# At most three gathers of result rows in flight at the end of a cross-attention and mixture-of-experts kernel

## The reference

```
x = x + xattn(layernorm(x), ctx)            # 32 heads of 16, rms-normalised q and k
xt = layernorm(x)                           # 2048 tokens x 512
gate = xt @ Wr + br;  ids = top_k(gate + gate_bias, 2);  probs = softmax(gate at ids)
u  = xt @ Wup[e] + bup[e]                   # for each of 7 experts, 512 x 512
g  = silu(u @ Wgate[e] + bgate[e]) * u
eo = g @ Wdown[e] + bdown[e]
out = sum over the token's two experts of probs * eo  +  the same three layers with Wsu, Wsg, Wsd
x  = x + out
```

## Time and profile before

| what | value |
| --- | --- |
| median of 3 runs | 1083.45 us (1082.43 to 1084.23) |
| span of the profiled execution, first to last instruction | 1096.4 us |
| PE busy | 1011.1 us, 92% of the span |
| DVE busy | 726.6 us, 66% |
| ACT busy | 475.6 us, 43% |
| POOL busy | 287.0 us, 26% |
| mean granted PE clock | 0.974 |

### The profile page before, as it was taken

The page is one execution under the profiler, slowest core; times in us unless marked ns, Lnnn a source line. Parts: engine busy times, 40 slices in busy tenths (PEclk is TensorE's granted clock), DMA queues, the critical chain, the costliest instruction groups (busy, mean ns, idle before and its releaser), DMA issues.

```text
span 1096.4 us, 20598 instructions
## 1 busy us (share of the span) xinstructions
PE 1011.1 (92%) x7368; PEld 791.9 (72%) x7369; DVE 726.6 (66%) x1686; ACT 475.6 (43%) x670; POOL 287.0 (26%) x194
## 2 busy tenths in 40 slices
PE   3699999998999989999699999999999999999776
PEld 3555556565555665555299899999999899999666
DVE  6677876756676675765456887547474774765378
ACT  2256556545666446656723324233333342432111
POOL 3434444432343433432100010110101010101552
PEclk9899999999999999999879999999999999999889
DMA  9430000010000100000131015424242433332564
GB/s 321 159 116 2 1 1 2 20 59 3 1 1 30 49 3 1 21 20 1 49 136 67 20 32 187 158 69 171 70 174 75 179 120 121 139 90 77 163 193 144
DMA packets 32636, 88.90 MB, mean 81 GB/s; under 512 B 5040, under 2 KB 6576, under 8 KB 29104
## 3 DMA queue, kind: packets, MB, share of 16 engines
q1 hardware_dynamic: 25680, 65.34, 16.3%
q0 software_dynamic: 6880, 22.55, 6.9%
HBM read 65.33 MB, written 22.54 MB: 80 GB/s over the span
## 4 chain that ended last, share of the span: by engine, by line
PE 44%; DVE 4%; another core or an unknown queue 2%; issue 1%; ACT 1%; DVEq 0%; ACTq 0%
PE u_ps L958 14%; PE y_ps L958 13%; PE z_ps L958 13%; PE xt_ps L971 2%; DVE x_sb L1391 1%; PE z_ps L952 1%; DVE g_sb L1332 0%; PE xt_ps L984 0%; DVE u_lo L1320 0%; DVE stats L1174 0%; DVE x_sb L1351 0%; DVE g_hi L1335 0%; ACT u_hi L1093 0%; DVE hot_row L1285 0%
## 5 line engine op out<-in xcount | busy, mean ns | idle before, releaser
L454 ACT ACTIVATE probs<-scores 128x1024 f32<-128x1024 f32 x256 | 247.8, 1030 | 164.7 <-PE scores L332 164.7
L204 POOL TENSOR_TENSOR rsqrt<-mean_sq,power 128x16 f32<-128x16 f32 (+1 forms) x69 | 193.0, 2798 | 312.2 <-DVE mean_sq L556 277.3
L958 PE MATMUL z_ps<-u_hi,w_sb 128*128 128x256 f32 x896 | 167.9, 285 | 2.0 <-DVE u_lo L1320 1.6
L958 PE MATMUL u_ps<-x_hi,w_sb 128*128 128x256 f32 x896 | 165.1, 282 | 4.4 <-issue 2.3
L958 PE MATMUL y_ps<-w_sb,g_hi 128*128 128x512 f32 x448 | 143.9, 402 | 12.6 <-DVE g_lo L1337 8.4
L1093 ACT ACTIVATE u_hi<-u_ps,b_ug 128x256 fp32r<-128x256 f32 x112 | 47.1, 472 | 237.0 <-PE u_ps L958 233.0
L958 PEld LDWEIGHTS u_ps<-x_hi,w_sb 128*128 128x128 f32 x896 | 140.4, 190 | 7.2 <-issue 3.8
L958 PEld LDWEIGHTS z_ps<-u_hi,w_sb 128*128 128x128 f32 x896 | 141.0, 190 | 2.9 <-DVE u_lo L1320 2.0
L344 PE MATMUL o_ps<-probs,v_sb 128*32 128x512 f32 x1024 | 136.4, 604 | 0.5 <-ACT probs L454 0.3
L958 PE MATMUL z_ps<-u_lo,w_sb 128*128 128x256 f32 x448 | 126.3, 282 | 0.1
L958 PE MATMUL u_ps<-x_lo,w_sb 128*128 128x256 f32 x448 | 125.9, 281 | 0.0
(11 more groups left out here) (149 smaller groups left out, 1774.4 us busy)
## 6 DMA issues: line engine op xcount, KB each, us to landing
w_raw<-w_all SPq DMA_DIRECT2D x27, 1024.0 KB, 6.9
y_dram<-y_sb SPq DMA_DIRECT2D x40, 256.0 KB, 2.1
ctx_sb<-ctx_t SPq DMA_DIRECT2D x4, 1024.0 KB, 7.3
out<-x_sb SPq DMA_DIRECT2D x16, 256.0 KB
y_dram<-zeros SPq DMA_DIRECT2D x1, 3584.0 KB, 23.6
x_sb<-x SPq DMA_DIRECT2D x1, 3072.0 KB, 20.1
xn_dram<-xn SPq DMA_DIRECT2D x12, 256.0 KB, 2.1
bd<-b_down SPq DMA_DIRECT2D x9, 256.0 KB, 3.4
```

The costliest lines, as they stand in the source:

```text
L204: nc.gpsimd.tensor_tensor(rsqrt[:, half, 0:width], mean_sq[:, half, 0:width], power[:, 0:width], ALU.pow).then_inc(rsqrt_ready, 1)
L454: nc.scalar.activation(probs[:, s % 2, 2 * a:2 * a + 2, :], scores[:, a], ACT.Exp, scale=float(HD) ** 0.5).then_inc(p_ready, 1)
L958: ins = nc.tensor.matmul(out_ps, stat[a], mov[b], start=(first and a + b == 0), stop=(last and a == 1), skip_group_check=True)
```

## The change

A constant FLYING = 3 is added. In `result(m)`, a gather with m of 3 or more first waits on POOL until gather m - 3 has landed, by that gather's own semaphore. The two `xg` gathers between m = 9 and m = 10 have no such wait. Nothing else is changed.

```diff
@@ -776,6 +776,7 @@
         index = sb("index", [P, 2], INT32)
         yg = w_raw[:].rearrange("p m c n -> p (m c) n")
         RING = 3 * DC
+        FLYING = 3
 
         def two_banks(name):
             return ctx.enter_context(nc.psum_tensor(name, [P, 2, 2, TS], FP32))
@@ -914,6 +915,9 @@
 
                 if m >= RING:
                     pool.wait_ge(added, m - RING + 1)
+                if m >= FLYING:
+                    before = m - FLYING
+                    pool.wait_ge(yg_loaded[before % RING], 16 * (before // RING + 1))
                 nc.gpsimd.indirect_dma_start(
                     out=yg[:, m % RING, :], out_offset=None, in_=y_dram,
                     in_offset=bass.IndirectOffsetOnAxis(
```

## The result

The changed kernel took 1090.65 us as a median of 20 runs (1088.83 to 1096.52), against 1084.16 us for the kernel before (20 runs, 1080.34 to 1090.80). The ratio is 1.0057, interval 1.0044 to 1.0071: slower by 0.6%, or 6.5 us. The forecast was no change, 1083.5 us within 1080.6 to 1086.8, and it was missed.

The account below looks back on a forecast made before the run. The prediction saw a late PE signal to ACT in the closing tiles, taken as hardly present in timed runs. Waits at 0, slip within slack and no stall removed summed to 0 us: 1083.5 us, range 1080.6 to 1086.8.

Parts of the forecast that it names:

- 29 waits at 0, a slip of 0 to 1 us behind 1.6 us of slack: Last stage: POOL's added waits cost nothing and later gathers slip less than their consumers' slack; 0 us in sum.
- L: Time from a gather's start on POOL to its landing; 3.7 to 4.2 us at first, 4.6 to 6 beside stores.
- the first burst: Result gathers m = 0 to 9 in the first closing tile; ten started, 1.7 outstanding, the limit just met.
- rival 2: At m = 3 to 9 and the `xg` pair, the limit paces gathers too slowly; 1085.3 to 1088.3 us, chance 0.20.
- the slip of m = 9: Delay of gather m = 9 under the limit, 3L - 11.6: nothing at 3.7, 1.0 us at 4.2, 3.4 at 5.
- slack of 2.0 us: First closing tile: m = 9 lands at 1036.2, its add starts at 1038.2 in an undisturbed run.
- From m = 14 ... POOL then runs ahead of DVE and the slack grows from tile to tile: Later gathers: the ring's wait on `added` lets POOL go on at once, since adds come 14 us earlier.
- The stall: Closing tiles: PE's `z_ready` reaches ACT 6 and 14 us late while gathers move; 14.4 to 16.7 us of the span.
- It comes with the recording: Claim that profiling causes the late signal, so timed runs hardly have it and nothing is there to be won.
- the subtraction: Profiled span 1096.4 us less timed median 1083.45: at least 12.95 us not in timed runs, at most 3.75 us of stall left.
- undisturbed span: Span of the kernel before without the late signal, put at 1079.7 to 1082.0 us.
- Rival 1: Closing tiles: timed runs have the late signal too and fewer gathers remove it; all gives 1079.7 us, chance 0.18.

Follow-up runs that it names:

- before_quiet: The kernel before, unedited, profiled in a later measurement; 1083.67 us, ratio 1.0010, span 1080.9 us.
- fly3_first: Kernel before plus the limit of three for m = 3 to 9 only; 1084.97 us, ratio 1.0016 to the kernel before.
- fly3_rest: Kernel before plus the limit of three from m = 10 on only; 1088.47 us (4 runs), ratio 1.0051 to the kernel before.
- the four repeats: The changed kernel, unedited, measured four more times beside the kernel before; 1090.17 to 1091.09 us, ratios 1.0049 to 1.0074.
- fly4: Also written F = 4: the changed kernel with at most four gathers in flight; 1096.91 us, ratio 0.9985 to the kernel before.
- F = 6: The changed kernel with at most six gathers in flight; 1098.24 us, ratio 0.9992 to the kernel before.
- pe_shift: Kernel before plus 96 semaphore instructions on PE at the start of the second stage, no limit; 1092.58 to 1098.60 us (4 runs), ratio 1.0111.
- before_again: The kernel before, unedited, in the measurement with the late signal; 1098.81 us, ratio 1.0003, span 1096.7 us.

## Why the prediction was wrong

**The step that failed** is the price of the limit: "29 waits at 0, a slip of 0 to 1 us behind 1.6 us of slack". It has two parts.

*L was mis-sized.* I took 3.7 to 4.2 us for the first burst, from bytes: 8.3 gathers' worth had moved by 1034, ten had started, so 1.7 were outstanding. In before_quiet the queue moved as much, 2.20 MB, and the landings of the same ten took 4.6 us at the median. A semaphore stands for a whole gather, and the mean of the bytes doesn't show when its last part lands. At a start every 1.25 us, the 4.9 us of the whole stage are 3.9 gathers in flight, so a limit of three binds. Under the limit the landings got shorter, 3.8 us at the median for the first ten, which is inside my range; the waits fell on the slow ones, as on m = 2 with 5.47 us in the chain. At L = 5 the text has 1.8 us for rival 2, and the first closing tile lost 2.0. That agreement is partly luck: the slip of m = 9 was 1.7 us, not 3L - 11.6 = 3.4, and it met the adds of m = 8 and 9 rather than the `xg` pair. Their slack of 2.0 us had been worked out with 3.3 us to landing; at 5.0 us it is gone, since 1032.79 + 5.0 is 1037.8, and the eighth add of before_quiet starts at about 1032.45 + 7 x 0.77 = 1037.8.

*The later bursts were left out.* "From m = 14 ... POOL then runs ahead of DVE and the slack grows from tile to tile" is true of the kernel before: in before_quiet m = 31 starts at 1067.20 and the last group of adds ends at 1075.78. It is false under the very limit being priced. A limit of three lets POOL go at L/3 plus its pause of 0.30 us, which is 1.7 us with the measured 4.3 us. The 56.22 us over 31 steps are 1.8 us each, against 1.49 before. The adds, four in a tile's first group and six or eight in the second, then catch up with POOL and wait. I had the number for it, "L is 4.6 to 6 us beside stores", and used it only as the upper end of the first burst. Rival 2 had the right mechanism with a place too narrow ("m = 3 to 9 and the `xg` pair"): fly3_first costs 0.12 to 0.16% and fly3_rest 0.51%. The end of my range stood on the first burst alone, so it was too low.

*A term missing from the sum*: 2.5 us of the 7.8 come from PE's clock after its idle time before the last z. In the four repeats and in fly3_rest that z takes 1.4 to 2.5 us more than 5.94.

**The stall.** "It comes with the recording" is refuted: before_quiet was profiled and has no stall. The time of an execution is its span plus 1.7 to 2.1 us with the stall and without: 1082.92 for a span of 1080.9, and 1098.72 for 1096.7. I had set the span of one measurement against the median of another. The Trainium skill's rule ("NOTIFIC — the notification-queue block", 7.1) that the path of the records holds its producer back explains no difference here. What the subtraction was used for held, by the times: the three runs of 1083.45 us agree with before_quiet, which has no such stall. My estimate of the undisturbed span, 1079.7 to 1082.0 us, is met by 1080.9, and by its pieces: DVE's eight adds foreseen at 1032.8, found at 1032.45 (z was taken to start at 1023.95, and the trace of the kernel before has it at 1023.71); `y_sb` foreseen at 1038.95, found at 1038.58.

**Rival 1** is not what the measurement of the change shows, since its kernel before had no stall. It has a true core: two in flight do take the stall away, at a price above it. F = 4 and F = 6 keep it (17.7 and 20.6 us of unnamed waits).

**The signs named.** POOL's new waits were there, mainly in the later bursts, as said, but 13 for 13.6 us and not a few. m = 9 came 13.37 us after m = 0 (11.6 to 12.6 said). Adds waited for gathers (none said). The profiled execution had no nameless wait (one said).

**Open.** What delays `z_ready` by 6 to 14 us in some measurements and never in others; whether three in flight avoid it; what F = 4 and F = 6 cost without it; why pe_shift cost 12 us. No version beat both kernels: fly4, the nearest, is at 0.9985 with an interval that reaches 1.0002, and only in the measurement with the late signal.

## What to carry to other kernels

Before a limit on transfers in flight is put in, take the time from issue to the semaphore of one such transfer in the busiest stretch, divide it by the limit, and compare this with the mean interval of issues that the whole stage needs, not with one burst's slack. Bytes moved don't give that time; the landings do. Look for the cost in the consumer's row: waits of the issuing queue are free until the consumer waits. And never subtract a span of one measurement from a median of another; ask for one execution's time and span together.

## What the runs showed of the hardware

- A gather of 128 rows of 2 KB lands after 3.3 us when nearly alone (the loop of before_quiet). In the last stage the median is 4.9 us without a limit (3.4 to 6.2), 4.3 us with three in flight, 3.8 us with two, and 3.6 us with three and no stores beside them, though the bytes alone give 1.37 us each.
- The same kernel on the same chip took 1098.8 us in one measurement (35 runs, 1095.57 or more) and 1083.9 us in another (22 of 23 runs, 1088.15 or less). In the traces the difference is an unnamed wait of ACT before `s_sb` while gathers move, 25.4 us in before_again; by the program the signal is PE's `z_ready`. With two in flight it was absent.
- After 4.45 us without work PE's next product ran at the 1.2 GHz level for its first 4.0 us: 8.43 us for 48 matmuls that took 5.94 at 2.4 GHz. The other traces with waits of 2.4 to 7.3 us before it have 7.33 to 8.43 us, those with 1.1 to 1.7 us have 5.93.
